# Masks of four attention pairs copied into PSUM by ScalarE, and counting instructions moved in TensorE's queue

## The chip, the core and the metric

The kernel runs on one core of a Trainium2 chip: TensorE (PE, with its weight loads shown apart as PEld), VectorE (DVE), ScalarE (ACT), GpSimd (POOL), and SyncE (SP), which issues transfers. The engines run side by side and meet at semaphores. The metric is the time of one execution on the device, in microseconds (us).

## What is computed

All matrices are float32. `x` has 16 sequences of 256 rows of 128. The first stage is causal attention with 16 heads of 8; the second is six layers of windowed attention (16 heads of 64, window 32) and a gated feed-forward block.

```python
# first stage, per sequence
q, k, v = proj(Wq), proj(Wk), proj(Wv)              # (16, 256, 8) each
scores = einsum('bhsd,bhtd->bhst', q, k)
scores = where(triu(ones((S, S)), k=1), -inf, scores)
attn = softmax(scores / sqrt(D)); out = einsum('bhst,bhtd->bhsd', attn, v)
x = x + out @ Wo.T
# second stage, six times
x = attn_layer(shift_tokens(x), ...) + x
x = ffn_layer(shift_tokens(x), ...) + x
```

## The kernel before

**First stage.** One step works on one sequence. Its 256 queries are two tiles of 128 (P). For a head the scores stand in one PSUM bank: columns 0 to 127 are tile 0 against keys 0 to 127, columns 128 to 383 are tile 1 against all 256 keys. The causal mask is needed in columns 0 to 127 and 256 to 383; columns 128 to 255 are all visible. The 16 heads are taken as 8 pairs, numbered 0 to 7, and a pair takes two neighbouring banks (`SCORE_BANK`). Three pairs of banks are shared by the eight pairs, in turn.

For a pair, TensorE (`a_scores`) first writes the mask into both banks with two bf16 matmuls (identity times mask, L1166), which start the accumulation, then adds the scores of tile 0 (two matmuls, L1170) and of tile 1 (two, L1173). VectorE takes the negated row maxima (`a_max`, L840 and L841), ScalarE the exponentials (`a_exp`, four activations, L561 and L562), TensorE transposes the exponentials in blocks of four heads (`a_turned`, L1181), ScalarE or VectorE copies the blocks out of PSUM (L568, L846), and TensorE sums the values (`a_value_sums`, L1193 and L1198). The steps are staggered: within one, TensorE computes pair 7 of sequence n-1, pairs 0 to 4 of n, the value sums of n-1, and then pairs 5 and 6 of n, with the transposes between them. The order on every engine is written out by hand in its `a_step`; steps 2 to 15 run as a loop of two steps (`attention_steps`), steps 0, 1 and 16 stand apart.

**Second stage.** 96 units (six layers by 16 sequences) in steps that overlap up to four units. TensorE's order is written out by `step` and unrolled (`stack_steps_straight`): no loop, so its instructions are a straight stream. In `scores` (L1373) a step issues 64 small matmuls twice, in `values` (L1341) 32 twice, in `output` (L1351) 16; `turn` (L1360) transposes, `project` (L1325) makes Q, K and V.

**Increments that place the code.** `fill(pe, i_fill, count)` puts `count` semaphore increments into TensorE's queue. Nothing waits for the semaphore `i_fill`; the increments only move what stands behind them in the instruction stream. 44 stand at the head of the second stage, ahead of the wait for the last sequence's value sums (L1396 and L1397); some one to five per step follow. `need_apart` is a wait followed by such an increment.

ScalarE starts with the guess of the first LayerNorm (L533 and L535). The mask's float32 form `causal_f` (256 columns: 128 zeros and the 128x128 mask) is loaded by SyncE; the semaphore `d_c` counts it and another constant, `wmask_f`.

Of the kernel before, what the change touches and what calls it, by code (L numbers as in the profile page):

```python
# [42 lines left out]
def fill(eng, counted, count):  # L43

    for _ in range(count):
        eng.sem_inc(counted, 1)


def need_apart(eng, idle, sem, value):


    need(eng, sem, value)
    eng.sem_inc(idle, 1)


def build(nc, x_in, wq_t, wk_t, wv_t, wo_t, wqkv, q_scale, k_scale, wo2, ln_g, ln_b, w1, b1, w2, b2,
          c_ident, c_winmask, c_causal, c_headmask, c_rot, out):
    with ExitStack() as ctx:
# [3 lines left out]
        def sem(name):  # L62
# [83 lines left out]

        names = ("d_x d_x2 d_wa d_wap d_rot d_c d_wq d_wk d_wv d_qks d_wo d_ln d_ff d_out i_const i_zero i_pad i_dve i_pool i_sp i_guess i_pe d_id d_wav d_hm "
                 "a_lnc a_lnr a_lnn a_xh a_xt a_xe a_qk a_qe a_ke a_km a_v a_ve a_s a_mx a_e a_t a_te "
                 "a_pv a_oe a_rc a_mu a_td i_slot a_on a_wo a_x1 b_lnc b_lnr b_lnn "
                 "s_x s_st s_xt s_xe s_pq s_pk s_pv s_sqq s_sqk s_rq s_rk s_fl s_lg s_iv s_nw s_hq s_hk "  # L150
                 "s_aq s_ak s_bq s_bk s_rot s_tr s_te s_mk s_sc s_mx s_sub s_exp s_sum s_rl s_pn s_T "
                 "s_o s_oe s_ve s_wo s_r1 d_sh s_lnc s_lnr s_lnn s_ln s_xn s_xne s_h s_gl s_g s_y s_xc "
# [1 line left out]
        S = {n: sem(n) for n in names.split()}  # L154
        (d_x, d_x2, d_wa, d_wap, d_rot, d_c, d_wq, d_wk, d_wv, d_qks, d_wo, d_ln, d_ff, d_out, i_const, i_zero, i_pad, i_dve, i_pool, i_sp, i_guess, i_pe, d_id, d_wav, d_hm,
         a_lnc, a_lnr, a_lnn, a_xh, a_xt, a_xe, a_qk, a_qe, a_ke, a_km, a_v, a_ve, a_s, a_mx, a_e, a_t, a_te,
         a_pv, a_oe, a_rc, a_mu, a_td, i_slot, a_on, a_wo, a_x1, b_lnc, b_lnr, b_lnn,
         s_x, s_st, s_xt, s_xe, s_pq, s_pk, s_pv, s_sqq, s_sqk, s_rq, s_rk, s_fl, s_lg, s_iv, s_nw, s_hq, s_hk,
         s_aq, s_ak, s_bq, s_bk, s_rot, s_tr, s_te, s_mk, s_sc, s_mx, s_sub, s_exp, s_sum, s_rl, s_pn, s_T,
         s_o, s_oe, s_ve, s_wo, s_r1, d_sh, s_lnc, s_lnr, s_lnn, s_ln, s_xn, s_xne, s_h, s_gl, s_g, s_y, s_xc,  # L160
# [16 lines left out]
        def attention_steps(eng, a_step):  # L177
            a_step(0, 0, True, False, False)
            a_step(1, 1, True, True, False)
            with eng.Fori(0, SEQS // 2 - 1) as k:  # L180
                for odd in range(2):
                    a_step(eng.snap(2 * k + (2 + odd)), odd, True, True, True)
            a_step(SEQS, 0, False, True, True)
# [7 lines left out]

        SCORE_BANK = {j: 2 * s for j, s in ((7, 0), (0, 1), (1, 2), (2, 0), (3, 1), (4, 2), (5, 1), (6, 2))}
        VALUE_BANK = 0

        TURN = {x: TR[s] for x, s in (("x", 0), ("01", 1), ("qk", 0), ("11", 1), ("12", 0), ("out", 1), ("20", 0), ("02", 1),
                                      ("30", 0), ("31", 1), ("32", 0), ("21", 1), ("22", 0), ("v", 1), ("00", 0), ("10", 1))}
# [321 lines left out]
        def _(act):  # L518
# [37 lines left out]
            def a_exp(n, j):  # L556

                need(act, a_mx, NPAIR * n + j + 1)
                for b, (g, k) in enumerate(pair_heads(j)):
                    h, bank = 4 * g + k, SCORE_BANK[j] + b  # L560
                    act.activation(E0[:, h, :], ps[:, bank, 0:P], ACT.Exp, bias=nmx[:, 0, h:h + 1])  # L561
                    last = act.activation(E1[:, h, :], ps[:, bank, P:P + SEQ], ACT.Exp, bias=nmx[:, 1, h:h + 1])  # L562
                last.then_inc(a_e, 1)

            def a_evac(n, b):

                need(act, a_t, turned(n, b))
                act.activation(block_home(b), block_seen(b), ACT.Copy).then_inc(a_te, 1)  # L568

            def a_step(n, par, head, mid, tail):  # L570
                if mid:
                    a_values(n - 1)
                if head:
                    rsqrt_guess(n, a_lnc, a_lnr, mv, lw)
                if mid:
                    a_evac(n - 1, "00")
                    a_evac(n - 1, "10")
                if head:
                    a_x_evac(n)
                if mid:  # L580
                    a_evac(n - 1, "01")
                if head:
                    a_qk_evac(n, par)
                if mid:
                    need(act, a_t, NBLK * (n - 1))
                    if isinstance(n, int) and n == 1:
                        act.wait_ge(i_zero, 2)
                        load_qkv(0, 0, d_wq)
                        load_qkv(0, 1, d_wk)
                        load_v(0, 0, d_wv)  # L590
                        load_v(0, 1, d_wv1)
                    a_exp(n - 1, 5)
                    a_exp(n - 1, 6)
                    a_exp(n - 1, 7)
                    a_evac(n - 1, "02")
                if head:
                    if mid:
                        need(act, a_t, turned(n - 1, "02"))
                    a_exp(n, 0)
                    a_exp(n, 1)  # L600
                    a_exp(n, 2)
                if tail:
                    rsqrt_guess(n - 2, b_lnc, b_lnr, mvb, lwb)
                if head:
                    a_exp(n, 3)
                    if mid:
                        need(act, a_t, turned(n - 1, "22"))
                    a_exp(n, 4)

            act.wait_ge(i_guess, 2)  # L610
            attention_steps(act, a_step)
            act.wait_ge(i_zero, 6)

# [520 lines left out]
        def _(pe):  # L1134
# [27 lines left out]

            def a_scores(n, j, par):
                bank = SCORE_BANK[j]
                for b in range(2):
                    mm(ps[:, bank + b, 0:3 * P].rearrange("p (a k) -> p a k", a=3)[:, 0:3:2, :], ident_h[:, :],  # L1166
                       causal[:, P:2 * P].unsqueeze(1).broadcast_to([P, 2, P]), start=True, stop=False, skip_group_check=True)
                for b, (g, k) in enumerate(pair_heads(j)):
                    r = slice(32 * g, 32 * g + 32)
                    mm(ps[:, bank + b, 0:P], AqT[r, par, 0:P], KM[r, par, k, 0:P], start=False, stop=True, skip_group_check=True)  # L1170
                for b, (g, k) in enumerate(pair_heads(j)):
                    r = slice(32 * g, 32 * g + 32)
                    last = mm(ps[:, bank + b, P:P + SEQ], AqT[r, par, P:SEQ], KM[r, par, k, :],  # L1173
                              start=False, stop=True, skip_group_check=True)
                last.then_inc(a_s, 1)
# [145 lines left out]
            def project(n, kind, part, par):  # L1321
                t, h = int(part[0]), int(part[1])
                at, done = (("Q", s_pq), ("K", s_pk), ("V", s_pv))[("Q", "K", "V").index(kind)]
                w0 = ("Q", "K", "V").index(kind) * INNER + 512 * h
                mm(home(kind + part), xsT[:, par, t * P:(t + 1) * P], Wqkv[:, w0:w0 + 512],  # L1325
                   start=True, stop=True).then_inc(done, 1)
# [61 lines left out]
            def step(n, u, par, live, layer):  # L1388
# [4 lines left out]
                begin = isinstance(n, int) and n == 0  # L1393
                loaded = 16 * (layer + 1)
                if begin:
                    fill(pe, i_fill, 44)  # L1396
                    pe.wait_ge(a_oe, SEQS)  # L1397
                if now:
                    turn_x(n)
# [95 lines left out]
                    output(n - 2, 1, 1)  # L1495
                if one:
                    project(n - 1, "V", "01", old)
                if now:
                    need(pe, s_n0, 2 * n + 1)
                    turn(n, "k01")  # L1500
                    need(pe, s_n0, 2 * n + 2)
                    need(pe, s_r1, n - 1)
                    if static:
                        need(pe, s_hk, nth(n, PARTS["K"], "10"))
                    turn(n, "q01")
                    need(pe, s_ve, nth(n - 1, PARTS["V"], "01"))
                    turn(n, "k00")
# [59 lines left out]
```

## Time and profile before

| | us |
|---|---|
| median of three executions | 3202.72 (3200.12 to 3204.0) |
| the profiled execution | 3200.21 |
| its span, first to last instruction | 3198.4 |
| PE busy | 3120.5 (98%) |
| DVE busy | 2874.1 (90%) |
| ACT busy | 2792.6 (87%) |
| POOL busy | 2683.4 (84%) |

Some 2 us of the profiled execution lie outside its span. Matmuls are pipelined, so busy PE is not PE at its peak. "issue" is time for which the profile shows no wait. The first stage ends at about 366 us; the second begins at 371.9 us.

### The profile page before, as it was taken

To read this page: it belongs to the slowest core of one execution; us is meant where nothing else is said; L and a number is where in the kernel's file an instruction comes from. 1 tells how busy PE (TensorE), PEld (TensorE's weight loads), DVE (VectorE), ACT (ScalarE), POOL (GpSimd) and SP (SyncE) were. 2 spreads that over 40 slices of the span, in tenths; PEclk is the share of its full clock that TensorE was granted. 3 is DMA by queue.
4 is the path that set the end of the run, shared out by engine and by line. 5 is a ranking of instruction groups with operands and counts; after the bars stand their busy time and mean duration, and the time that the engine had idled before them with its cause. 6 is when DMAs were issued, how large, how long until landed. Compare 5 with 4: busy or idle time off the path is not lost.

```text
span 3198.4 us, 128703 instructions
## 1 busy us (share of the span) xinstructions
PE 3120.5 (98%) x51488; PEld 2274.6 (71%) x51488; DVE 2874.1 (90%) x5656; ACT 2792.6 (87%) x5313; POOL 2683.4 (84%) x1798
## 2 busy tenths in 40 slices
PE   8999699999999999999999999999999999999996
PEld 5777467777677777777777777777777777777775
DVE  6999789999999999899999999999999999999994
ACT  5777489999999999899999999999999999999994
POOL 2000299999999999999999999999999999999992
PEclk9999899999999999999999999999999999999998
DMA  2000011111221112211112211112211112211112
GB/s 71 1 0 0 0 28 42 39 36 38 62 55 37 35 41 51 55 43 39 42 42 54 52 41 42 40 36 54 58 42 38 35 39 63 55 36 35 41 42 55
DMA packets 127301, 128.93 MB, mean 40 GB/s; under 512 B 62380, under 2 KB 75824, under 8 KB 126832
## 3 DMA queue, kind: packets, MB, share of 16 engines
q1 hardware_dynamic: 123232, 112.38, 14.4%
q10 hardware_dynamic: 3600, 9.50, 0.9%
q8 instruction: 391, 6.41, 0.9%
q14 instruction: 78, 0.64, 0.1%
HBM read 19.04 MB, written 2.10 MB: 7 GB/s over the span
## 4 chain that ended last, share of the span: by engine, by line
PE 95%; DVE 1%; DMA 1%; issue 1%; ACT 1%; POOL 0%; SPq 0%; ACTq 0%; DVEq 0%; POOLq 0%
PE ps L1325 30%; PE ps L1351 11%; PE ps L1360 10%; PE ps L1373 9%; PE ps L1341 9%; PE ps L1317 9%; PE ps L1383 5%; PE ps L1181 3%; PE ps L1173 2%; PE ps L1170 2%; PE ps L1193 1%; PE ps L1166 1%; PE ps L1206 1%; PE ps L1301 1%; PE ps L1294 1%
## 5 line engine op out<-in xcount | busy, mean ns | idle before, releaser
L1325 PE MATMUL ps<-Wqkv,xsT 128*128 128x512 f32 x2304 | 1084.7, 600 | 7.8 <-DMA Wqkv<-ffn_Wqkv 3.4
L458 POOL TENSOR_TENSOR area<-area,tab 128x512 f32<-128x512 f32 x768 | 961.3, 1283 | 44.6 <-ACT area L646 44.0
L1325 PEld LDWEIGHTS ps<-Wqkv,xsT 128*128 128x128 f32 x2304 | 400.8, 191 | 350.4 <-issue 241.4
L480 POOL TENSOR_TENSOR area<-area,lsum 128x1024 f32<-128x1024 f32 x192 | 365.8, 1905 | 132.2 <-DVE lsum L944 130.4
L465 POOL TENSOR_TENSOR area<-area 128x1024 f32<-128x1024 f32 x192 | 451.3, 2377 | 0.5 <-DVE area L1003 0.5
L646 ACT ACTIVATE area<-ps 128x512 f32<-128x512 f32 x768 | 444.2, 594 | 7.4 <-PE ps L1325 7.1
L465 POOL TENSOR_TENSOR AQb<-AQb,area 128x1024 f32<-128x1024 f32 x192 | 450.1, 2366 | 0.1
L651 ACT ACTIVATE area<-area 128x1024 f32<-128x1024 f32 x384 | 396.5, 1065 | 0.0
L1351 PE MATMUL ps<-Wo,area 128*128 128x128 f32 x3072 | 368.5, 278 | 0.5 <-ACT area L696 0.5
L473 POOL TENSOR_TENSOR area<-area,inv 128x1024 f32<-128x1024 f32 x192 | 361.6, 1906 | 3.9 <-DVE inv L989 3.9
L1351 PEld LDWEIGHTS ps<-Wo,area 128*128 128x128 f32 x3072 | 350.2, 192 | 9.3 <-ACT area L696 0.6
L1373 PE MATMUL ps<-kT,area 64*32 64x64 f32 x24576 | 309.4, 226 | 8.0 <-issue 5.5
L1373 PEld LDWEIGHTS ps<-kT,area 64*32 64x32 f32 x24576 | 272.3, 105 | 43.1 <-issue 27.3
L1341 PE MATMUL ps<-BD,area 64*64 64x96 f32 (+1 forms) x12288 | 296.6, 240 | 1.2 <-ACT area L676 1.0
L1317 PE MATMUL ps<-xnT,W 128*128 128x256 f32 (+1 forms) x1152 | 295.7, 394 | 1.3 <-ACT xnT L702 1.3
L663 ACT ACTIVATE area<-ps 128x512 f32<-128x512 f32 x384 | 225.1, 596 | 63.6 <-PE ps L1325 61.2
L1341 PEld LDWEIGHTS ps<-BD,area 64*64 64x64 f32 x12288 | 260.4, 133 | 25.1 <-issue 2.3
L398 POOL TENSOR_TENSOR area<-AkT,slotmask 128x1024 f32<-128x1024 f32 x16 | 30.3, 1895 | 294.4 <-ACT AkT L548 294.4
L928 DVE TENSOR_REDUCE mx<-ps 128x8 f32<-128x512 f32 x384 | 254.1, 683 | 21.4 <-PE ps L1373 13.7
L1360 PEld LDWEIGHTS ps<-ident,area 128*128 128x128 f32 x1536 | 179.9, 142 | 122.7 <-issue 100.2
L623 ACT ACTIVATE area<-area 128x1024 f32<-128x1024 f32 x192 | 203.3, 1059 | 71.9 <-DVE area L934 71.9
L676 ACT ACTIVATE area<-ps 128x512 f32<-128x512 f32 x384 | 229.9, 599 | 37.8 <-PE ps L1360 37.8
(124 smaller groups left out, 6551.2 us busy)
## 6 DMA issues: line engine op xcount, KB each, us to landing
BD<-area SPq DMA_DIRECT2D x1440, 64.0 KB
Wqkv<-ffn_Wqkv ACTq DMA_DIRECT2D x12, 512.0 KB, 4.7
x2s<-x2s SPq DMA_DIRECT2D x96, 56.0 KB, 2.1
Wo<-ffn_Wo SPq DMA_DIRECT2D x6, 512.0 KB, 4.9
Wqkv<-ffn_Wqkv ACTq DMA_DIRECT2D x12, 256.0 KB, 3.1
W<-ffn_W SPq DMA_DIRECT2D x6, 341.0 KB
x2s<-x2s SPq DMA_DIRECT2D x96, 7.5 KB, 3.2
x2s<-x2s SPq DMA_DIRECT2D x96, 0.2 KB, 2.5
```

The lines of the kernel that those rows point to most:

```text
L458: pool.tensor_tensor(b4[:, :, here], q4[:, :, there], s4[:, :, here], ALU.mult).then_inc((s_bq, s_bk)[j], 1)
L465: pool.tensor_tensor(AQ[t][:, col], AQ[t][:, col], BQ[:, col], ALU.add).then_inc(s_rot, 1)
L473: pool.tensor_tensor(a3, a3, inv0[:, j * HEADS:(j + 1) * HEADS].unsqueeze(2).broadcast_to([P, HEADS, DH]), ALU.mult).then_inc(s_n0, 1)
L480: pool.tensor_tensor(p3, p3, lsum[:, 1, :].unsqueeze(2).broadcast_to([P, HEADS, 2 * WIN]), ALU.mult).then_inc(s_pn, 1)
L646: act.activation(QH[:, at:at + 512], home(kind + part), ACT.Copy).then_inc(kept, 1)
L651: act.activation(SQ[:, col], QH[:, col], ACT.Square).then_inc((s_sqq, s_sqk)[j], 1)
L1317: last = mm(home(f"h{c}")[0:m, half * SEQ:(half + 1) * SEQ], W1[:, half * FF + f0:half * FF + f0 + m], xnT[:, :], start=True, stop=True)
L1325: mm(home(kind + part), xsT[:, par, t * P:(t + 1) * P], Wqkv[:, w0:w0 + 512], start=True, stop=True).then_inc(done, 1)
L1341: last = mm(ps[DH * k:DH * k + DH, VALUE_HOME[g][b], q0:q0 + WIN * wide], V[par][keys, t, h * DH:(h + 1) * DH], BD[keys, t, 0:wide, place( ...
L1351: last = mm(home("out")[:, t * P:(t + 1) * P], oT[:, c, t * P:(t + 1) * P], Wo[:, c, :], start=(t == 0 and c == 0), stop=(c == PAIRS - 1), ...
L1360: last = tp(home(x)[:, c * P:(c + 1) * P], AQ[t][:, at:at + P], ident[:, :])
L1373: last = mm(ps[32 * w:32 * w + 32, SCORE_HOME[k], 2 * WIN * c:2 * WIN * (c + 1)], qT[half, c, 32 * w:32 * w + 32], kT[half, c, k0:k0 + 2 * ...
```

## The change

The masks of pairs 0, 2, 4 and 5 are copied by ScalarE for every sequence but the first: one activation per pair writes 2 x 384 columns (mask, zeros, mask) into the pair's two banks, and `a_scores` waits for it (`a_mk`) in place of its two mask matmuls. The 384 columns come from `causal3`, built at the start of ScalarE's queue by two activations behind a wait for `d_c` and ahead of everything else there. The 44 increments at the head of the second stage are gone; 64 stand near the end of its step 0 and 64 near the end of its step 1, ahead of the transposes of k01.

```diff
+        BY_COPY = (0, 2, 4, 5)
+        causal3 = G[:, :, :].rearrange("p c n -> p (c n)")[:, 0:3 * P]
...
+            def a_mask(n, j):
+                bank = SCORE_BANK[j]
+                need(act, a_e, NPAIR * n + {0: -2, 2: 0, 4: 2, 5: 4}[j])
+                act.activation(ps[:, bank:bank + 2, 0:3 * P], causal3.unsqueeze(1).broadcast_to([P, 2, 3 * P]),
+                               ACT.Copy).then_inc(a_mk, 1)
...
             act.wait_ge(i_guess, 2)
+            act.wait_ge(d_c, 16 * N_CONST)
+            act.activation(causal3[:, 0:P], causal_f[:, P:2 * P], ACT.Copy).then_inc(a_c3, 1)
+            act.activation(causal3[:, P:3 * P], causal_f[:, :], ACT.Copy).then_inc(a_c3, 1)
+            act.wait_ge(a_c3, 2)
             attention_steps(act, a_step)
...
             def a_scores(n, j, par):
                 bank = SCORE_BANK[j]
-                for b in range(2):
+                copied = j in BY_COPY and not (isinstance(n, int) and n == 0)
+                if copied:
+                    need_apart(pe, i_pe, a_mk, len(BY_COPY) * (n - 1) + BY_COPY.index(j) + 1)
+                for b in range(0 if copied else 2):
...
                 if begin:
-                    fill(pe, i_fill, 44)
                     pe.wait_ge(a_oe, SEQS)
...
                     project(n - 1, "V", "01", old)
+                if n < 2:
+                    fill(pe, i_fill, (64, 64)[n])
                 if now:
                     need(pe, s_n0, 2 * n + 1)
                     turn(n, "k01")
```

In ScalarE's queue the copies stand in the middle of the exponentials. First the piece of the loop body before, from the exponentials of pair 7 of the old sequence to those of pair 0 of the new one (L561 and L562 are exponentials, L568 the copy of block 02):

```order
L561 ACTIVATE area<-ps,nmx 128x128 [waits a_mx]
L562 ACTIVATE area<-ps,nmx 128x256
L561 ACTIVATE area<-ps,nmx 128x128
L562 ACTIVATE area<-ps,nmx 128x256
L568 ACTIVATE area<-ps 128x4x128 [waits a_t]
L561 ACTIVATE area<-ps,nmx 128x128 [waits a_mx,a_t]
L562 ACTIVATE area<-ps,nmx 128x256
```

And the same piece now, in the changed kernel's line numbers (L570 is the mask's copy, L563 and L564 the exponentials, L576 the copy of block 02):

```order
L570 ACTIVATE ps<-G 128x2x384 [waits a_e]
L563 ACTIVATE area<-ps,nmx 128x128 [waits a_mx]
L564 ACTIVATE area<-ps,nmx 128x256
L563 ACTIVATE area<-ps,nmx 128x128
L564 ACTIVATE area<-ps,nmx 128x256
L576 ACTIVATE area<-ps 128x4x128 [waits a_t]
L570 ACTIVATE ps<-G 128x2x384 [waits a_e]
L563 ACTIVATE area<-ps,nmx 128x128 [waits a_mx,a_t]
L564 ACTIVATE area<-ps,nmx 128x256
```

The copy for pair 0 stands ahead of the exponentials of pair 7, the copy for pair 2 ahead of those of pair 0; the other two follow the exponentials of pairs 2 and 4.

On TensorE, pair 0 in the loop body before, behind the transposes of block 20 (L1181) and ahead of those of block 02:

```order
L1181 MATMUL ps<-ident,area 128x128 [waits a_td]
L1181 MATMUL ps<-ident,area 128x128 x3
L1166 MATMUL ps<-causal,ident_h 128x2x128 [waits a_qe,a_km]
L1166 MATMUL ps<-causal,ident_h 128x2x128
L1170 MATMUL ps<-area,AqT 128x128 x2
L1173 MATMUL ps<-area,AqT 128x256 x2
```

Now (L1204 is the transpose, L1193 and L1196 are the scores):

```order
L1204 MATMUL ps<-ident,area 128x128 [waits a_td]
L1204 MATMUL ps<-ident,area 128x128 x3
L1193 MATMUL ps<-area,AqT 128x128 [waits a_mk,a_km,a_qe]
L1193 MATMUL ps<-area,AqT 128x128
L1196 MATMUL ps<-area,AqT 128x256 x2
```

The two mask matmuls are gone, and the first score matmul also waits for the copy.

## Rows read from the trace of the kernel before

**Rows 1.** The page: engines, instruction queue, chain by engine, one group, one issue
```profile
PE 3120.5 (98%) x51488; PEld 2274.6 (71%) x51488; DVE 2874.1 (90%) x5656; ACT 2792.6 (87%) x5313; POOL 2683.4 (84%) x1798
...
q8 instruction: 391, 6.41, 0.9%
...
PE 95%; DVE 1%; DMA 1%; issue 1%; ACT 1%; POOL 0%; SPq 0%; ACTq 0%; DVEq 0%; POOLq 0%
...
L651 ACT ACTIVATE area<-area 128x1024 f32<-128x1024 f32 x384 | 396.5, 1065 | 0.0
...
wmask_f<-const SPq DMA_DIRECT2D x1, 64.0 KB, 2.1
```

**Rows 2.** The chain of one first-stage step: start, us, what
```profile
150.88 1.86 PE ps L1193 x32
...
154.21 0.22 PE ps L1166 x2
...
170.74 0.22 PE ps L1166 x2
...
172.45 1.86 PE ps L1193 x32
```

**Rows 3.** Waits of ACT, 60 to 318 us: total us, times, longest
```profile
ACT area L561 <- DVE nmx L841: 35.8, 53, 2.0
ACT area L568 <- PE ps L1181: 19.2, 24, 0.9
```

**Rows 4.** Timeline of ACT in that step: start, us, instruction, idle before
```profile
153.75 0.38 ACT L553 ACTIVATE area<-ps 128x256 f32<-128x256 f32 x1
...
169.95 0.31 ACT L533 ACTIVATE lwb<-mvb,consts 128x2 f32<-128x2 f32 x1
...
172.59 0.37 ACT L561 ACTIVATE area<-ps,nmx 128x128 f32<-128x128 f32 x1 [2.00 <-DVE nmx L841]
```

**Rows 5.** The mask copies of the second stage (L690): ns min/median/max, first and last
```profile
L690 ACT ACTIVATE ps<-wmask_f x384: 578/595/603, 396.8 to 3146.4; 128x512 f32<-128x512 f32 x192
```

**Rows 6.** Timeline of the kernel's start, SP's queue and ACT
```profile
3.66 0.43 SPq L290 DMA_DIRECT2D wmask_f<-const  x1
...
4.30 0.29 ACT L533 ACTIVATE lw<-mv,consts 128x2 f32<-128x2 f32 x1 [1.80 <-DVE mv L804]
```

**Rows 7.** The 44 increments: ns min/median/max, first and last start
```profile
L46 PEldq EVENT_SEMAPHORE  x44: 51/51/51, 365.0 to 371.7; - x44
```

**Rows 8.** The chain between the two stages
```profile
367.14 4.77 issue
```

**Rows 9.** Timeline of PE at the end of second-stage steps 0 and 1
```profile
397.80 1.11 PE L1360 MATMUL ps<-ident,area 128*128 128x128 f32 x4 [11.36 <-POOL area L473]
...
421.34 2.08 PE L1325 MATMUL ps<-Wqkv,xsT 128*128 128x512 f32 x2
424.93 1.11 PE L1360 MATMUL ps<-ident,area 128*128 128x128 f32 x4 [1.51 <-POOL area L473]
```

**Rows 10.** Waits of PE, 480 to 3100 us
```profile
PE ps L1373 <- issue: 5.2, 5, 1.5
```

**Rows 11.** Timeline of PE in second-stage step 15
```profile
820.75 0.68 PE L1373 MATMUL ps<-kT,area 64*32 64x64 f32 x42
822.59 1.08 PE L1373 MATMUL ps<-kT,area 64*32 64x64 f32 x86 [1.16 <-issue]
```

**Rows 12.** Transfers that begin in 820.1 to 820.2 us: packets, MB, share
```profile
q8 instruction: 1, 0.02, 60.2%
```

**Rows 13.** Transfers that begin in 646.3 to 646.5 us, step 9
```profile
q8 instruction: 1, 0.02, 29.2%
```

**Rows 14.** Timeline of PE in step 9
```profile
648.72 1.48 PE L1373 MATMUL ps<-kT,area 64*32 64x64 f32 x128
650.14 3.84 PE L1351 MATMUL ps<-Wo,area 128*128 128x128 f32 x32
```

**Rows 15.** Transfers that begin in 649.9 to 651 us, step 9
```profile
q8 instruction: 1, 0.02, 5.8%
```

More of the change, by code:

```diff
@@ L148, in build @@
                  "a_lnc a_lnr a_lnn a_xh a_xt a_xe a_qk a_qe a_ke a_km a_v a_ve a_s a_mx a_e a_t a_te "
-                 "a_pv a_oe a_rc a_mu a_td i_slot a_on a_wo a_x1 b_lnc b_lnr b_lnn "
+                 "a_pv a_oe a_rc a_mu a_td a_mk a_c3 i_slot a_on a_wo a_x1 b_lnc b_lnr b_lnn "
                  "s_x s_st s_xt s_xe s_pq s_pk s_pv s_sqq s_sqk s_rq s_rk s_fl s_lg s_iv s_nw s_hq s_hk "
@@ L156, in build @@
          a_lnc, a_lnr, a_lnn, a_xh, a_xt, a_xe, a_qk, a_qe, a_ke, a_km, a_v, a_ve, a_s, a_mx, a_e, a_t, a_te,
-         a_pv, a_oe, a_rc, a_mu, a_td, i_slot, a_on, a_wo, a_x1, b_lnc, b_lnr, b_lnn,
+         a_pv, a_oe, a_rc, a_mu, a_td, a_mk, a_c3, i_slot, a_on, a_wo, a_x1, b_lnc, b_lnr, b_lnn,
          s_x, s_st, s_xt, s_xe, s_pq, s_pk, s_pv, s_sqq, s_sqk, s_rq, s_rk, s_fl, s_lg, s_iv, s_nw, s_hq, s_hk,
@@ L593, in a_step @@
                     a_exp(n - 1, 6)
+                    if head:
+                        a_mask(n, 0)
                     a_exp(n - 1, 7)
                     a_evac(n - 1, "02")
+                    if head:
+                        a_mask(n, 2)
                 if head:
@@ L601, in a_step @@
                     a_exp(n, 2)
+                    if mid:
+                        a_mask(n, 4)
                 if tail:
@@ L608, in a_step @@
                     a_exp(n, 4)
+                    if mid:
+                        a_mask(n, 5)
             act.wait_ge(i_guess, 2)
+            act.wait_ge(d_c, 16 * N_CONST)
+            act.activation(causal3[:, 0:P], causal_f[:, P:2 * P], ACT.Copy).then_inc(a_c3, 1)
+            act.activation(causal3[:, P:3 * P], causal_f[:, :], ACT.Copy).then_inc(a_c3, 1)
+            act.wait_ge(a_c3, 2)
             attention_steps(act, a_step)
```

## Prediction

> **What bounds the kernel now.** I read the page first, then the chain and the waits of one first-stage step, then the timeline of the places that the edits touch. The page names TensorE: busy 98% of the span and 95% of the chain that ended last, with VectorE at 90% and ScalarE at 87% [rows 1]. In the first stage the chain runs from one value-sum block (L1193) at 150.88 us to the next at 172.45 us, so a step takes 21.57 us, and the two masks of a pair are 0.22 us of it [rows 2]. TensorE is nearly gapless there. ScalarE is not: over twelve steps its exponentials wait 35.8 us for VectorE's maxima and its block copies 19.2 us for TensorE, 4.6 us a step from these two alone [rows 3]. What the reader is to see is that this slack isn't free to use where it falls: the largest piece, 2.00 us, stands ahead of the exponentials of pair 3, while the copies are placed before and behind it [rows 4].
>
> In the second stage TensorE is the chain again, except in its first two steps, where it waits for GpSimd: 11.36 us at the end of step 0, only 1.51 us at the end of step 1 [rows 9].
>
> **The change part by part**, against the profiled execution (3200.21 us, 1.8 us more than its span; the median shown is 2.5 us above it).
>
> *Start: +2.4 us.* ScalarE's first activation begins at 4.30 us and the chain goes through it to the first scores. Now the wait for `d_c` comes first. It counts both constants; the second is issued at 3.66 us [rows 6] and such an issue lands 2.1 us later [rows 1], at 5.76 us. Behind it stand two short copies and a wait for their ends, about 0.9 us (a 128x256 copy takes 0.38 us [rows 4], and they overlap a little). So the first LayerNorm guess starts near 6.7 us. Nothing hides it: VectorE and TensorE have nothing else yet. Bounds: 1.5 (the wait alone) and 2.8.
>
> *Masks off TensorE: -3.3 us.* Four pairs by 0.22 us are 0.88 us a step, over the 15 steps that copy 13.2 us. Against it stand two waits. A copy writes 768 columns. The nearest rows are 0.595 us for 512 columns into PSUM [rows 5] and 1.065 us for 1024 [rows 1]; between them lies 0.83 us, of which some 0.05 overlaps the next instruction. Pairs 0 and 2: ScalarE has idle time ahead of the exponentials of pair 7, of block 02 and of pair 0, so the copies push little.
> Pair 4: its copy follows the exponentials of pair 2, which leave ScalarE at 169.95 us (L533 starts there [rows 4]). Two copies have by then used up the idle time of this stretch, so that point comes earlier only with TensorE, by two masks: 169.51; the copy is written at 170.33. TensorE reaches pair 4 at 170.74 less 0.44, 170.30 [rows 2]. With the semaphore and the increment behind it (an increment takes up to 6.7/43 = 0.156 us of the queue [rows 7]) I take 0.2 us of waiting.
> Pair 5: the exponentials of pair 3 follow VectorE's maxima at 172.59 us, which follow TensorE's last transposes, and those of pair 4 leave ScalarE at 153.75 + 21.57 = 175.32 us [rows 4]. The copy is written at 176.15. TensorE reaches pair 5 at 154.21 + 21.57 = 175.78 us [rows 2], or, counted from the same transposes, 0.22 earlier for pair 4's mask and 0.2 later for its wait: 175.76. It waits 0.4 us. What is queued behind this wait is all of TensorE: the transposes of block 10, pair 6 and the next sequence's first transposes; and behind the copy on ScalarE stand the value copy and block 00, which the next LayerNorm transposes need.
> So 0.88 - 0.2 - 0.4 = 0.28, and I leave 0.22 a step for the increments: 3.3 us. Bounds: all 13.2 gained if a copy costs as little as 0.595; and a loss of 4.5 (0.3 a step) if it costs 1.065, when both waits grow by 0.24, the copies of pairs 0 and 2 overrun their slack, and ScalarE's delay returns to the maxima.
>
> *The 44 increments go: -4.8 us.* They run from 365.0 to 371.7 us, 0.156 us apart [rows 7], though each is only 51 ns long. The value sums that the queue then waits for are gathered by 367.14 us, and 4.77 us of the chain are "issue" [rows 8]. That time goes; next in line is VectorE's gather, already counted. Bounds: 4 and 6.5 (TensorE also sits idle for less, so its clock may stay at its upper level).
>
> *64 increments in step 0: nothing.* 64 x 0.156 = 10.0 us against 11.36 us of waiting for GpSimd [rows 9]. If that cover shrank by 1.4 us, the rest would show.
>
> *64 in step 1: +5.5 us.* Here the same 10.0 us meets little. The queue reaches them when V01 is issued, about 421.4 us, and leaves them at 431.4; the transposes would have begun at 424.93 us [rows 9]. That is 6.5 us later, less about 1 us of waits for GpSimd that vanish behind it. GpSimd needs Q of unit 2 for its next work, so it is late too, and nothing gives the time back. Bounds: 3 and 8.
>
> *Where the code's pieces end: +4 us.* The instruction queue brings 391 packets of 6.41 MB, 16.4 KB each [rows 1]. A second-stage step is about 1024 instructions by the code (a float32 matmul is two passes of a weight load and a matmul), 96 of them about 98,000 of 64 bytes: four packets a step, so the seams lie at the same four places in every step. One shows itself: in step 15 the second scores stop behind 42 of their 128 matmuls and go on at 822.59 us [rows 11], 2.5 us after the packet of 820.1 [rows 12]. Five such stops cost 5.2 us [rows 10]. In step 9 the packet of 646.3 is there in time [rows 13].
> The edit moves the code. Per copied pair four instructions leave (two mask matmuls, two loads) and one comes (wait and increment together); twelve pairs stand in the code (step 1 and two loop bodies): -36. The increments are 128 for 44: +84. Net +48, 24 matmuls with their loads. So the seam in the scores falls behind 19 of 128, near 648.9 us in step 9, and the next one, until now in the quiet end of the step, 128 pairs on: behind 19 of the 32 in `output`, 650.14 + 19 x 0.12 = 652.4 us [rows 14]. That is 3.5 us between seams. In step 9 the packet begins 0.8 us behind its seam (649.9 [rows 15]), and in step 15 its instructions ran 2.5 us after it began: 3.3 us. The margin is next to nothing, in every step. I take four steps' worth of 1.0 us (5.2/5). Bounds: 0, and 15 if one step in six stops like that.
>
> The Trainium skill speaks against this term: the page "Runtime: NRT & Kernel Launch", section on instruction fetch mechanics, says that refilling goes in blocks of 256 instructions and that crossing a block's edge is mostly hidden. This trace agrees on the block and contradicts "hidden" in the five stops. By the rule the term would be zero.
>
> Sum: 2.4 - 3.3 - 4.8 + 0 + 5.5 + 4 = +3.8: 3204.0 us for the profiled execution, 3206.5 us as a median. A measurement of this kernel tells about 0.2%, 6.4 us, from no change; so my forecast is no change, leaning to slower.
>
> **Rivals.**
> A, the masks come off whole. For it: 4.6 us a step of idle ScalarE [rows 3]. Against it: where the idle time stands. Then 2.4 - 13.2 - 4.8 + 5.5 + 0 = -10.1: 3192.6 us.
> B, ScalarE's copy sets the pace. From about 0.95 us per copy the waits for pairs 4 and 5 exceed the 0.88 saved; at 1.065 the stage loses 4.5 instead of gaining 3.3. For it: no row shows two banks written in one activation. Against it: 0.595 for 512 columns. 3202.7 + 2.4 + 4.5 - 4.8 + 5.5 + 4 = 3214.3 us, slower.
> C, the seam in `output` stops TensorE often: 15 instead of 4: 3217.5 us, slower. It decides where packets begin more than about 1 us behind their seam.
> D, the fetch is always hidden in normal steps: 0 instead of 4: 3202.5 us. The traces give it less than the forecast, since the five stops are there.
> That the code does not do what it says I can exclude: the order shows the masks gone and the copies in place.
>
> **How the numbers follow.** Forecast 0.32, A 0.19, B 0.15, C 0.18, D 0.16. Faster by over 0.2% is A (0.19) and a little of D; slower is B and C; the rest is within. The range leaves out the far ends of A and C: 3194 to 3218 us. The likeliest case by itself spans 3201 to 3211.
>
> **What would show it.** In the profile of the changed kernel: the first activation of the LayerNorm guess near 6.7 us and the first scores 2.4 us later; a first-stage step of 21.3 to 21.4 us, with TensorE waiting for the mask copies at pairs 4 and 5 and not at 0 and 2; copies of 0.8 us; the second stage's first transposes less than 1 us behind VectorE's gather; no new wait at the end of step 0, and in step 1 the transposes some 6 us behind the last projection's start plus what they took before; "issue" waits on L1351 (`output`). I am wrong if a step takes 20.7 us (A), 21.9 us (B), if waits on `output` sum to over 8 us (C) or none are there (D), or if step 1 loses less than 3 us.

## The result, and the profile after

The changed kernel takes 3219.44 us (median of five, 3214.5 to 3228.08) against 3202.72: ratio 1.0054, 95% interval 1.0040 to 1.0068. It is slower, and lies outside the predicted range. The profiled execution, 3228.08 us, is the highest of the five (span 3226.3 against 3198.4), so it holds more loss than the median does, while the profiled execution before lies 2.5 us under its median.

The page after, beside [rows 1]: TensorE is busy 8.6 us more with 120 instructions fewer, and the instruction queue brings as many packets. New is the idle time of `output` (L1374, before L1351, where it was 0.5).

```profile
PE 3129.1 (97%) x51368; PEld 2279.2 (71%) x51368; DVE 2872.6 (89%) x5656; ACT 2827.6 (88%) x5375; POOL 2680.7 (83%) x1798
...
q8 instruction: 391, 6.41, 0.8%
...
L1374 PE MATMUL ps<-Wo,area 128*128 128x128 f32 x3072 | 378.7, 279 | 11.5 <-issue 9.4
```

Cut at the first and last value sums and at the transposes that open each second-stage step, the two profiled executions differ so:

| stretch | before, us | after, us | difference |
|---|---|---|---|
| start to first scores | 12.29 | 14.54 | +2.25 |
| from there to the first value sums | 30.65 | 42.14 | +11.5 |
| the next period | 21.57 | 23.06 | +1.5 |
| 13 periods (21.57, then 21.39) and the last | 298.47 | 296.08 | -2.4 |
| last value sums to second stage | 8.89 | 4.20 | -4.7 |
| its step 0 | 29.33 | 29.08 | -0.25 |
| its step 1 | 27.13 | 32.12 | +5.0 |
| its step 2 | 27.05 | 26.02 | -1.0 |
| steps 3 to 94, 92 of them (mean 28.730, then 28.920) | 2643.1 | 2660.6 | +17.5 |
| the rest | 99.9 | 98.4 | -1.5 |

Two places carry the loss: 17.5 us in the second stage's steps, and 13 us between the first scores and the second value sums.

ScalarE at the start: the two activations that build the blocks, and the first guess at 6.54 us (I had said 6.7), which began at 4.30 us before [rows 6].

```profile
5.89 0.31 ACT L628 ACTIVATE G<-causal_f 128x128 f32<-128x128 f32 x1 [3.39 <-DMA wmask_f<-const]
6.11 0.40 ACT L629 ACTIVATE G<-causal_f 128x256 f32<-128x256 f32 x1
6.54 0.30 ACT L535 ACTIVATE lw<-mv,consts 128x2 f32<-128x2 f32 x1
```

TensorE in step 1, start, us, instruction, idle before: the same score matmuls (L1193) last 0.80, then 0.49, then again 0.80 us.

```profile
23.55 0.80 PE L1193 MATMUL ps<-area,AqT 32*128 32x128 f32 x4
...
36.63 0.49 PE L1193 MATMUL ps<-area,AqT 32*128 32x128 f32 x4
...
39.02 0.63 PE L1204 MATMUL ps<-ident,area 128*128 128x128 f32 x4 [0.88 <-DVE area L866]
40.88 0.80 PE L1193 MATMUL ps<-area,AqT 32*128 32x128 f32 x4 [1.23 <-ACT ps L570]
...
56.68 3.64 PE L1216 MATMUL ps<-area 128*32 128x256 f32 x32
```

The same time by windows (us, busy time of PE, PEld, DVE, ACT, POOL, granted clock, DMA share, GB/s):

```profile
37.00:40.00 3.00, 1.78 (x16) 1.00 (x12) 2.77 (x7) 2.68 (x9) 1.11 (x1) 0.99 0.93 352
40.00:50.00 10.00, 9.12 (x43) 6.33 (x44) 4.86 (x9) 6.50 (x18) 0.00 (x0) 0.50 0.11 41
50.00:60.00 10.00, 10.00 (x63) 6.00 (x65) 4.64 (x11) 4.68 (x13) 0.00 (x0) 0.50 0.01 2
60.00:63.00 3.00, 3.00 (x51) 2.19 (x44) 1.54 (x4) 1.34 (x4) 0.00 (x0) 0.93 0.00 0
```

TensorE waits twice, 0.88 us for a block copy and 1.23 us for the first mask copy, and from then on its granted clock is 0.50, the 1.2 GHz level, for 20 us. In the kernel before the same place has one wait, of 1.19 us, and the clock stays at 1.00 (2.4 GHz):

```profile
33.13 0.66 PE L1181 MATMUL ps<-ident,area 128*128 128x128 f32 x4 [1.19 <-ACT area L562]
```

```profile
37.00:40.00 3.00, 3.00 (x29) 2.11 (x27) 2.96 (x6) 2.45 (x9) 0.00 (x0) 1.00 0.01 3
40.00:50.00 10.00, 9.96 (x125) 6.85 (x121) 8.24 (x20) 5.66 (x18) 0.00 (x0) 1.00 0.01 2
```

The column alone would mislead: it reads 1.00 from the start too, while the matmuls go at the slow pace until 25 us (before) or 36 us (after). A stretch is slow when either the column or the duration of one form says so.

The first stage's steady step, around pair 4 (L1193 and L1196 scores, L1180 value projection), and the copies (ns min/median/max):

```profile
183.84 1.09 PE L1204 MATMUL ps<-ident,area 128*128 128x128 f32 x8
185.21 0.49 PE L1193 MATMUL ps<-area,AqT 32*128 32x128 f32 x4 [0.27 <-issue]
185.50 0.63 PE L1196 MATMUL ps<-area,AqT 32*128 32x256 f32 x4
186.06 0.71 PE L1180 MATMUL ps<-Wa,xhT 128*128 128x128 f32 x4
```

```profile
L570 ACT ACTIVATE ps<-G x60: 809/847/873, 39.8 to 360.4; 128x768 f32<-128x768 f32 x60
```

The profile names no releaser for the 0.27 us ahead of pair 4's scores ("issue"), but the pair's copy on ScalarE ends just before them, at 185.10 us, and in a later run (e11) the same kind of wait is put down to the copy:

```profile
184.23 0.87 ACT L570 ACTIVATE ps<-G 128x768 f32<-128x768 f32 x1
```

From a pair's preceding transposes to the next instructions behind its scores, the edit saves 0.22 us for pair 2, 0.05 for pair 5, 0.02 for pair 0 and loses 0.13 for pair 4 (186.06 - 183.84 = 2.22 against 2.09): 0.16 of the step's 0.18.

The seam in `output`, here one of its longer stops, and the waits of TensorE from 480 to 3100 us [rows 10] (total us, times, longest):

```profile
1328.87 2.27 PE L1374 MATMUL ps<-Wo,area 128*128 128x128 f32 x18
1331.63 1.83 PE L1374 MATMUL ps<-Wo,area 128*128 128x128 f32 x14 [0.48 <-issue]
```

```profile
PE ps L1374 <- issue: 9.0, 25, 1.1
PE ps L1396 <- issue: 4.8, 4, 1.6
```

From its first matmul to the next instruction behind it, `output` takes 21.7 us more in the 92 steps than before, and over 0.05 us more in 55 of them. The 25 listed waits are 9.0 us of that; the rest is in gaps too short for the list.

The transposes at the ends of steps 0 and 1 [rows 9]:

```profile
405.68 1.12 PE L1383 MATMUL ps<-ident,area 128*128 128x128 f32 x4 [11.34 <-POOL area L475]
```

```profile
438.84 2.79 PE L1383 MATMUL ps<-ident,area 128*128 128x128 f32 x12 [7.52 <-issue]
```

TensorE's granted clock is at the half here in both kernels. Before, that stretch begins late in step 1 and reaches 3 us into step 2; after, more of it lies inside step 1 (first line before, second after, up to the start of step 2):

```profile
421.00:428.30 7.30, 5.04 (x46) 2.83 (x34) 7.01 (x12) 3.86 (x7) 7.19 (x6) 0.51 0.01 3
429.00:441.20 12.20, 4.68 (x38) 2.99 (x25) 10.28 (x17) 4.00 (x6) 12.17 (x8) 0.50 0.07 18
```

### The profile page after: what moved, and what is told of

The parts are those of the page before. It is cut to its first block, busy times and chain, and to the rows that moved or that the text cites. A ratio compares the mean times of both kernels' runs of the same rounds, so it can differ in the third digit from the quotient of the medians.

```text
span 3226.3 us, 128684 instructions
## 1 busy us (share of the span) xinstructions
PE 3129.1 (97%) x51368; PEld 2279.2 (71%) x51368; DVE 2872.6 (89%) x5656; ACT 2827.6 (88%) x5375; POOL 2680.7 (83%) x1798
## 4 chain that ended last, share of the span: by engine, by line
PE 95%; issue 1%; DVE 1%; ACT 1%; DMA 1%; POOL 0%; SPq 0%; ACTq 0%; DVEq 0%; POOLq 0%
PE ps L1348 31%; PE ps L1374 12%; PE ps L1383 10%; PE ps L1396 9%; PE ps L1364 9%; PE ps L1340 8%; PE ps L1406 5%; PE ps L1204 3%; PE ps L1196 2%; PE ps L1193 2%; PE ps L1216 1%; PE ps L1229 1%; PE ps L1324 1%; PE ps L1317 1%; PE ps L1171 1%
## 5 line engine op out<-in xcount | busy, mean ns | idle before, releaser
L1374 PE MATMUL ps<-Wo,area 128*128 128x128 f32 x3072 | 378.7, 279 | 11.5 <-issue 9.4
L1374 PEld LDWEIGHTS ps<-Wo,area 128*128 128x128 f32 x3072 | 354.4, 192 | 26.4 <-issue 17.1
L1364 PEld LDWEIGHTS ps<-BD,area 64*64 64x64 f32 x12288 | 260.4, 133 | 25.7 <-issue 2.8
```

Source lines behind the costliest of these rows:

```text
L1364: last = mm(ps[DH * k:DH * k + DH, VALUE_HOME[g][b], q0:q0 + WIN * wide], V[par][keys, t, h * DH:(h + 1) * DH], BD[keys, t, 0:wide, place( ...
L1374: last = mm(home("out")[:, t * P:(t + 1) * P], oT[:, c, t * P:(t + 1) * P], Wo[:, c, :], start=(t == 0 and c == 0), stop=(c == PAIRS - 1), ...
```

## The experiments

Each is compared with the kernel before on the same chip (not all ran on one chip; the medians before lie between 3202.54 and 3204.27 us); a ratio has its 95% interval. Where two numbers stand for increments, they are those of step 0 and step 1. "Mean" is that of steps 3 to 94.

**e1: the second stage's code back in its place.**

```diff
-                    fill(pe, i_fill, (64, 64)[n])
+                    fill(pe, i_fill, (64, 16)[n])
```

> The changed kernel with 64 increments in step 0 and 16 in step 1 instead of 64 and 64. Together with the 36 instructions that the masks took out this puts the second stage's code where it stood in the kernel before. Theory 1 (the seams between the instruction packets cost 17 us in the second stage, 0.19 us a step): steps 3 to 95 fall back to a mean of 28.73 us, and step 1 loses at most 1 us instead of 5.0; 3219.4 - 17 - 4 = 3198 us, 3195 to 3202. Theory 2 (the second stage is slower for another reason than where its code is cut): the mean stays at 28.92 us and only step 1 gives something back, 3215 us.

Measured 3203.37 us (12 runs), ratio 1.0007 (0.9999 to 1.0016). The mean is 28.714 us and step 1 takes 27.41 us. So the 48 increments in step 1 cost both the longer steps and the loss of step 1: by the medians 16 us together, by the two profiled runs 24 (92 x 0.206 and 4.7). Theory 2 is out. The clock still fell in step 1: the first value sums began at 55.33 us.

**e2: the same shift in the kernel before.** 48 more increments where step 0 waits.

```diff
                 if one:
                     project(n - 1, "V", "01", old)
+                if begin:
+                    fill(pe, i_fill, 48)
```

> The kernel before with 48 more increments at the end of the second stage's step 0, where TensorE waits 11.4 us for GpSimd: nothing else than the code's place behind them changes, by the same 48 instructions as in the changed kernel. Theory 1 (seams): the mean of steps 3 to 95 rises from 28.73 to 28.92 us, +17 us, 3220 us (3215 to 3224). Theory 2: 3203 us, within 2.

Measured 3215.34 us, ratio 1.0042 (1.0029 to 1.0054), 12.8 us; mean 28.916 us, the changed kernel's. TensorE waits in `output` (L1351):

```profile
PE ps L1351 <- issue: 10.4, 28, 1.1
PE ps L1373 <- issue: 5.3, 5, 1.6
```

Step for step against the kernel before (the same weight loads, averaged over all 92 steps), everything up to `output` begins within 0.06 us of before, but for one pair of transposes that begins 0.20 us earlier; between the 18th and the 20th of its 32 weight loads 0.24 us come in and stay, and the step ends 0.19 us later. The shift alone makes the steps as long as in the changed kernel.

**e3: the masks alone.** 44 increments at the head as before, 36 in step 0.

> The masks copied as in the changed kernel, with ScalarE's wait for the constants at the start, but 44 increments at the head of the second stage as before, and 36 in its step 0 (behind a wait for GpSimd) to make up for the 36 instructions that are gone: the second stage as before, the first as changed. Theory 1 (the first stage's two parts are a start 2.3 us later and 0.18 us a step gained over 14 steps): 3202.7 + 2.3 - 2.6 = 3202.4 us. Theory 2 (the later start also shifts the stretches in which TensorE runs at its lower clock, up to 13 us in the first two steps): between 3202 and 3216 us, differing more from run to run than the kernel before does.

Measured 3209.99 us, ratio 1.0027 (1.0017 to 1.0038). A period is 21.39 us, as in the changed kernel; mean 28.752 us. The clock is at the half from 38 to 55 us and the first value sums begin at 53.15 us. Theory 2: the first stage as changed is a loss (7.5 us by the medians), not a gain.

**e4: the start alone.** The wait and the two builds in the kernel before.

> The kernel before with ScalarE's wait for the constants and the two copies that build the three-block mask at the start, and nothing else (the masks are made by TensorE as before, the built block is not used). Theory 1 (a delay is a delay): 3202.7 + 2.3 = 3205 us. Theory 2 (a later start changes when TensorE's clock reaches its upper level and whether it falls again): first value sums up to 11 us later than the delay explains, up to 3216 us in single runs.

Measured 3207.66 us (11 runs), ratio 1.0016 (1.0007 to 1.0025): 5.1 us for a start 2.1 us later. No half clock in step 1, but the first value sums begin at 48.41 us, 5.5 later than before. In e2, where the start is untouched, they begin at 46.63. The time at which TensorE first reaches its fast pace differs between executions: the kernel before, e2, e8, e9 and e10 have the same first stage, and it is 25 us in the kernel before and in e8, 34 to 35 us in the three others, with the first value sums at 42.94 and 42.95 against 46.63, 46.89 and 46.34. So a single profile can't price the start, and a difference of some 3.5 us ahead of the first value sums can be chance. The interval of e4 (2.2 to 8.0 us) holds the plain delay.

**e5 to e7: which part of the first stage.** e5 leaves sequence 1's masks to TensorE; e6 builds the block between the exponentials of step 0; e7 does both.

```diff
-                copied = j in BY_COPY and not (isinstance(n, int) and n == 0)
+                copied = j in BY_COPY and not (isinstance(n, int) and n < 2)
...
                     a_exp(n, 0)
+                    if not mid:
+                        act.wait_ge(d_c, 16 * N_CONST)
+                        act.activation(causal3[:, 0:P], causal_f[:, P:2 * P], ACT.Copy).then_inc(a_c3, 1)
```

> As the run e1, but the masks of sequence 1 are made by TensorE too, so that copies begin with sequence 2; the increments are 64 and 4, which keeps the second stage's code where it was. In e1 and e3 and in the changed kernel the first copy of step 1 comes late (ScalarE issues four transfers ahead of it), TensorE waits 1.2 to 1.5 us for it right behind another wait of about 1 us, and for the next 20 us its clock is at the half. Theory 1 (this wait brings the clock down): the drop goes, first value sums near 45 to 47 us, 3203.4 - 9 = 3194 us. Theory 2 (the clock falls because the start is later by 2.3 us): the drop stays, 3203 us.

> As the run e1 (64 and 16 increments), but the three-block mask is built between the exponentials of step 0, where ScalarE waits 0.77 us for each pair's maxima, not at the start. Theory 1 (the wait for the copy brings the clock down): the drop at 37 to 57 us stays, only the start comes back, 3203.4 - 2.2 = 3201 us. Theory 2 (the late start does): the drop goes, 3203.4 - 2.2 - 9 = 3192 us.

> Both edits: masks of sequence 1 by TensorE, the three-block mask built in step 0, increments 64 and 4. Against the kernel before it keeps the gain of 0.17 us a step over 13 steps (2.2) and of the increments moved from the head into step 0's wait (4.7), with no late start and no lower clock in step 1: 3202.5 - 6.9 = 3195.6 us; 3193 to 3198. If the 4.7 is given back in the second stage's first steps, 3200 us.

e5: 3195.16 us, ratio 0.9971 (0.9958 to 0.9983). e6: 3199.05 us, 0.9989 (0.9980 to 0.9999). e7: 3191.72 us, 0.9969 (0.9957 to 0.9981), 11.7 us below the kernel before (6 to 14 by the interval) and the lowest median of all runs, though not to be told from e5 or e11. Its profiled span is 11.8 us shorter: 2.2 us of that by the first value sums of the last sequence, 4.7 between the stages, and the rest mainly in step 0 (1.8) and behind the start of the last step (3.1), where less time lies at the half clock. (The code of e5 and e7 stands 4 instructions further than in the kernel before, not 0 as I had said, and in e11, e12 and e14 4 to 6: the rare stop in the second scores comes behind 40 or 39 matmuls in their traces, not 42. The means, 28.729 to 28.764, show no harm.) In e6 the clock still fell from 37 to 54 us, though the start was at its old place; in e5 and e7 it didn't. So it is the copies of sequence 1, not the late start. What the fall costs is best read from two profiles whose fast pace begins at the same time, 26.5 us: the first value sums begin at 50.96 us in e6 and 43.53 in e7, and the period behind them takes 22.61 against 21.40 us, together 8.6 us. TensorE in e7 at that place: one wait, and the score matmuls behind it stay at 0.49 us.

```profile
33.72 0.66 PE L1209 MATMUL ps<-ident,area 128*128 128x128 f32 x4 [1.19 <-ACT area L564]
34.21 0.38 PE L1194 MATMUL ps<-causal,ident_h 128*128 128x256 bf16 x2
34.52 0.49 PE L1198 MATMUL ps<-area,AqT 32*128 32x128 f32 x4
```

**e8: a sweep of the place.** 16 more increments every six steps, in the kernel before.

```diff
+                if isinstance(n, int) and n % 6 == 4:
+                    fill(pe, i_fill, 16)
```

> The kernel before with 16 more increments at the end of steps 4, 10, 16, ..., 94 of the second stage: every six steps the code is shifted by 16 more instructions, 256 in all. The steps in which they stand lose up to 2.5 us (16 x 0.156) each; the other five of each six show what a shift is worth, against the same steps of the kernel before. Theory 1 (a seam in `output` costs 0.18 us a step, one elsewhere less): steps shifted by 48 are 0.19 us longer, those in which no seam lies in `output` within 0.05 us of before. Theory 2 (every shift away from the tuned place costs the same): all shifts cost 0.1 to 0.2 us.

Measured 3320.83 us. Steps against the same steps before, us, leaving out those of the increments; ten of the fifteen shifts:

| shift | 16 | 32 | 48 | 64 | 96 | 128 | 176 | 208 | 224 | 240 |
|---|---|---|---|---|---|---|---|---|---|---|
| lowest | -0.20 | -0.61 | +0.06 | +0.73 | +2.31 | -0.26 | +0.68 | +2.42 | -0.28 | -0.02 |
| highest | +0.22 | 0.00 | +0.77 | +1.06 | +3.68 | +2.49 | +1.35 | +2.91 | +4.72 | +3.57 |

Both theories were too small: the kernel before stands in a narrow good place (shifts of 16 and 32 cost nothing), and the worst places cost over ten times the 0.19 us a step that the change lost.

**e9 and e10: one bad place, and a whole packet,** with 96 and 256 more increments in step 0.

> The kernel before with 96 more increments in the second stage's step 0. In the sweep e8 the steps shifted by 96 instructions were 2.3 to 2.5 us longer than before. Theory 1 (the cost hangs on where the seams stand, nothing else): the mean of steps 3 to 95 is 28.73 + 2.4 = 31.1 us, 92 x 2.4 = 220 us more, 3420 us. Theory 2 (the sweep's cost came from its own repeated increments): under 0.3 us a step, below 3235 us.

> The kernel before with 256 more increments in step 0, one whole packet. Theory 1 (only the place of the seams counts, and it repeats after 256 instructions): the mean of steps 3 to 95 is 28.73 us again; step 0 loses what the wait for GpSimd doesn't hide, 256 x 0.156 - 11.4 = 28.5 us: 3202.7 + 28.5 = 3231 us. Theory 2 (a longer stream costs by its length): the mean is 28.9 us or more, 3248 us.

e9: 3484.49 us (two runs), ratio 1.0878 (1.0854 to 1.0903), mean 31.676 us, a step 0.5 us longer than the sweep had let me expect. The waits from 480 to 3100 us, and one step:

```profile
PE ps L1373 <- issue: 179.6, 83, 2.8
```

```profile
640.45 1.43 PE L1373 MATMUL ps<-kT,area 64*32 64x64 f32 x122
644.40 0.31 PE L1373 MATMUL ps<-kT,area 64*32 64x64 f32 x6 [2.51 <-issue]
```

The seam now cuts the second scores behind 122 of 128, and TensorE stops there in nearly every step. The seam before it is 128 matmuls back, in `values`, some 1.5 us earlier (estimated from the rows of those blocks: 6 of 64 in 1.47 us, 122 of 128 in 1.42). The start times of the queue's packets show why that is too soon: from 400 us on, in all eighteen traces, no two of them begin less than 3.2 us apart. e10: 3226.33 us, ratio 1.0068 (1.0051 to 1.0085), mean 28.748 us. A shift by 256 instructions gives the old steps back, and only step 0 is longer (55.13 us). So the length of the stream costs nothing beyond step 0, its cut does.

**e11: pair 4's masks back to TensorE.**

```diff
-        BY_COPY = (0, 2, 4, 5)
+        BY_COPY = (0, 2, 5)
```

> As the run e7, but pair 4's masks stay with TensorE: copies for pairs 0, 2 and 5, and 62 increments in step 0 (none in step 1), so that the second stage's code stands where it did. In the changed kernel's trace, from a pair's preceding transposes to its following ones, the copy saves 0.22 us for pair 2, 0.05 for pair 5, 0.02 for pair 0, and loses 0.13 for pair 4 (TensorE waits longer than its two masks took). Theory 1 (the waits add up pair by pair): a step gains 0.29 instead of 0.17 us, 13 x 0.12 = 1.6 us less than e7: 3190 us. Theory 2 (the step is set by ScalarE's total work, of which a copy is 0.83 us): the gain grows by more, 0.4 us a step, 3188.5 us.

Measured 3195.13 us (12 runs), ratio 0.9972 (0.9963 to 0.9982); not to be told from e7. A period is 21.34 us against 21.37 in e7 (means of 13): pair 4's wait is gone, but pair 5 now waits as long.

```profile
156.58 0.49 PE L1198 MATMUL ps<-area,AqT 32*128 32x128 f32 x4 [0.27 <-ACT ps L572]
```

Both theories were too hopeful.

**e12: one copy in sequence 1,** that for pair 0, in e7.

> As the run e7, but in sequence 1 the one copy for pair 0 is made too (the one behind ScalarE's four transfer issues, for which TensorE waited 1.2 to 1.5 us in e1, e3 and the changed kernel); increments 64 and 7. Theory 1 (this one wait brings TensorE's clock down): a drop to the half of 14 to 20 us comes back between 35 and 60 us, 3191.7 + 9 = 3200 us. Theory 2 (it takes all four copies of that step): no drop, 3193 us.

Measured 3204.65 us (10 runs), ratio 1.0001 (0.9992 to 1.0010), 13 us above e7, or 12 when each is set against the kernel before on its own chip. Against e15, whose first stage is that of e7 and whose fast pace begins nearly as late (33 and 34 us), the first value sums begin 7.2 us later and the period behind them is 2.2 us longer, together 9.4. One copy is enough: waits of 0.88 and 1.39 us, and then the half clock.

```profile
36.63 0.63 PE L1209 MATMUL ps<-ident,area 128*128 128x128 f32 x4 [0.88 <-DVE area L871]
38.64 0.49 PE L1198 MATMUL ps<-area,AqT 32*128 32x128 f32 x4 [1.39 <-ACT ps L572]
...
42.89 0.80 PE L1198 MATMUL ps<-area,AqT 32*128 32x128 f32 x4
```

**e13 and e14: the transfer issues moved.** In the first, the `if n == 1` block with ScalarE's four transfers goes behind `a_exp(n, 4)` of its step. The second adds the late build and takes `BY_COPY = (0, 2, 5)`.

> As the run e1 (64 and 16 increments, mask built at the start, copies from sequence 1 on), but ScalarE's four transfer issues of step 1 stand at the end of its step instead of ahead of the exponentials of pair 5. Theory 1 (TensorE's clock falls in step 1 because those issues, 1.2 us, hold up the exponentials and then the first copy): the two waits of about 1 us go, no half clock between 36 and 60 us, 3203.4 - 9 - 1 = 3193 us. Theory 2 (any copy in sequence 1 starves TensorE): the drop stays, 3202 us.

> All that the runs point to: the mask built in step 0 and not at the start, the four issues at the end of ScalarE's step 1, copies for pairs 0, 2 and 5 from sequence 1 on, increments 68 and 3, which keep the second stage's code where it was before. Theory 1: e7's 3191.7 less 1 us (the wait of 1.2 us in step 1) less 13 x 0.05 (pair 4 not copied): 3190 us. Theory 2 (a first stage with no wait of its own leaves the rest as it is, but the times of the clock's changes differ from run to run by more than that): not to be told from e7, 3188 to 3196.

e13: 3201.18 us (12 runs), ratio 0.9991 (0.9981 to 1.0002); e14: 3202.46 us (12 runs), 0.9990 (0.9979 to 1.0000). My theory of the issues fell: they lengthen the second wait (0.63 and 0.65 us here, 0.89 to 1.50 with the issues in their old place), but don't make it. In e13's profile TensorE still waits 0.88 us for VectorE and then 0.65 us for the copy, and the clock falls as before:

```profile
38.91 0.63 PE L1204 MATMUL ps<-ident,area 128*128 128x128 f32 x4 [0.88 <-DVE area L866]
40.18 0.80 PE L1193 MATMUL ps<-area,AqT 32*128 32x128 f32 x4 [0.65 <-ACT ps L570]
```

e13's twelve times fall into two halves, 3193.8 to 3199.0 us (mean granted clock 0.992 to 0.994) and 3203.4 to 3206.2 (0.989 to 0.991). With the shorter wait the clock may fall in some executions only; profiles of both kinds would be needed to show it. e14's profile has the two waits (0.87 and 0.63 us) and the half clock too. The intended best version is worse than e7, which has no copy in sequence 1.

**e15 and e16: do the terms add up?** e15 is e7 with 64 and 52 increments, e16 the changed kernel again.

> The run e7 with 64 and 52 increments, which put the second stage's code where the changed kernel has it, and most of its increments into step 1. Theory 1 (the changed kernel = this first stage, which gains 12 us, plus the drop in step 1 and the late start, 11 us, plus the seams and the increments of step 1): 3191.7 + 17 (seams by the profiles) + 4.6 = 3213 us; if the seams are worth what the medians of e2 show, 12.8, 3209 us. Theory 2 (the losses do not add, the later second stage hides part): 3203 us or less.

> The changed kernel once more, beside the others: a second profile, to tell its fixed losses (steps of the second stage) from those that differ from run to run (when TensorE's clock rises at the start, whether it falls in step 1). Theory 1: 3219 us, mean of steps 3 to 95 again 28.92 us, the drop in step 1 again there. Theory 2 (the profiled run, 8.7 us above its median, was special): the mean nearer 28.87 us, and the drop not always there.

e15: 3227.25 us, ratio 1.0082 (1.0067 to 1.0096), mean 29.089 us. That was a miss with a cause: the code came to stand 52 instructions further than in the kernel before, not 48, and the four more make 0.17 us a step. The stop now stands behind 16 matmuls of `output`, not 18. The wait in `output` doubled against the changed kernel's 9.0 us in 25 places:

```profile
PE ps L1379 <- issue: 20.7, 53, 0.9
```

So e15 doesn't test the sum; it shows how steep the cost is there. e16: 3228.7 us (four runs, 3216.43 to 3230.82), ratio 1.0067 (1.0048 to 1.0087); mean 28.944 us, half clock from 40 to 61 us again, first value sums at 56.65. The first profile was not a special one: both losses are there in both.

## Why the prediction was wrong, point by point

Two steps failed: the first stage was priced from its steady step alone, and the seam was put at four steps' worth of stops.

- *Start +2.4*: 2.24 us, right as a delay; whether it costs more by way of the clock, e4's 5.1 us with its wide interval can't say.
- *Masks off TensorE -3.3*: 0.18 us a step instead of 0.22; TensorE waits at pair 4 (0.27) as said, less than said at pair 5 (0.10), and 0.12 at pair 0, where I had excluded a wait. The copy was well bounded (0.847 for my 0.83). **The step that failed is behind it: I priced 15 steps alike.** Step 1 is different, because TensorE already waits there once and ScalarE's queue is late. I looked at the copies in the steady step only. Behind one more wait the clock went to its lower level, and step 1 with the period behind it lost 13 us. Not all of that is the copies': by e6 against e7 and e12 against e15 the fall costs 8.6 to 9.4 us, and the other 4 are about what a late fast pace costs (36 us in this profile, 25 before), which e2, e9 and e10 show too, with the first stage of the kernel before. In all eight profiles with a copy in sequence 1 (the changed kernel, e1, e3, e6, e12, e13, e14, e16) the clock fell there, in none of the ten others (before, e2, e4, e5, e7 to e11, e15). That the copies do it is shown; that it is their wait, and not something else about them, is argued from its place just ahead of the fall, since no run has the wait without a copy. My rivals had it nowhere, since I had read TensorE's clock for the gap between the stages alone.
- *The 44 increments go -4.8*: 4.7 us, right.
- *64 in step 0: nothing*: right, the wait for GpSimd is 11.34 us as before.
- *64 in step 1: +5.5*: 5.0 us, of which 1.0 came back in step 2, which I had excluded. Of the half-clock stretch that step 2 began with before, 3 us, only half is left.
- *Where the code's pieces end: +4*: 17.5 us in the profiled run, 12.8 by e2's medians. The place was right: I said behind 19 of the 32 matmuls in `output`, it is behind 18, as 42 - 24 should have told me. **The size was not, and this is the second step that failed.** I counted on a few stops of 1.0 us, as rare as those of [rows 10]; there are 25 that the profile lists, 9.0 us in all, and `output` is longer by over 0.05 us in 55 of 92 steps. I had worked out a margin of nothing "in every step" and then priced it at four steps. A margin near zero means that what differs a little from step to step decides, and here that was a small loss in most steps. (The margin can be worked out again: up to the stop it is 110 score matmuls in 1.2 us and 18 of `output` in 2.1, 3.3 us between the seams by my estimate from their rows, not 3.5; the 21.7 us are 0.24 a step, so the packet is late by about that on average.) That is rival C in mechanism and size (15 us), and its sign, waits on `output` over 8 us, came true.
- The Trainium skill's rule (page "Runtime: NRT & Kernel Launch", section on instruction fetch mechanics: crossing a block's edge is mostly hidden) held in the places the kernel before uses, five stops apart, and not elsewhere: e9 shows 179.6 us of waits at one edge, and e10 confirms the block of 256.

Rival A fell (a step gained 0.18, not 0.88 us), B fell by its size, D by e1 and e2. The sum with the measured sizes is 2.2 + 13 - 2.4 - 4.7 - 0.3 + 5.0 - 1.0 + 17.5 - 1.5 = 27.8 us for the profiled run, its whole difference. The median is 16.7 us above the one before, and in e16 25.7. How far the seams differ between executions (12.8 by e2's medians, 17.1 by its profile) stays open.

## What to carry to other kernels

Price an edit in the prologue's steps apart from the steady step: there TensorE has waits already, and a second one beside them was followed by a loss of about six times its length at the lower clock (8.6 us behind 1.49, 9.4 behind 1.39). In a long unrolled stream, treat every added or removed instruction ahead of it as a change to all that follows: work out where each seam falls, and if two come to lie as close in time as here (3.3 to 3.5 us left no margin, 1.5 us in e9 a stop in nearly every step), make up for the shift where the queue idles. Re-measure such a place after any edit. The version to keep is e7: late build, no copy in sequence 1, increments moved into step 0's wait.

## What the runs showed that I had not expected

- Where the code stands is worth up to 280 us here (e9 against before, medians 3484.49 and 3204.27), for 96 instructions that do nothing. Four instructions are worth 0.17 us a step (28.920 and 28.944 at a shift of 48, 29.089 at 52).
- A further wait of 0.63 to 1.50 us close behind one of 0.87 to 1.19 us was followed by 14 to 21 us at the lower clock level, in eight of eight profiles; the one wait alone by none, in ten of ten. The fall cost 8.6 to 9.4 us.
- The packets of the instruction queue never began less than 3.2 us apart from 400 us on, in eighteen traces; at e9's seam, where 256 instructions run in about 1.5 us, TensorE stopped for 1.8 to 2.8 us.
- The time at which TensorE's matmuls first reach the fast pace differs between executions: it lies between 25 and 28 us in five of the eighteen profiles, between 32 and 38 in thirteen. It is 25 us in the kernel before and 34 in e10, which is the same program up to the second stage. In e11, also late, a block that took 1.13 us in the kernel before takes 1.91 (first line before, second e11). By itself that moved the first value sums from 42.94 to 46.34 us (e10).

```profile
28.72 1.13 PE L1151 MATMUL ps<-xhT,Wa 128*128 128x256 f32 x4
31.34 1.91 PE L1176 MATMUL ps<-xhT,Wa 128*128 128x256 f32 x4
```
